# A recurrent and a deformable convolution stage on one core: bank order of the sampling tiles, a column-wise second depthwise convolution, and five linear chunks finished by ScalarE

## The reference

```
x = x + lstm_block(group_norm(x))      # over the 64 rows, both directions, 16 hidden units, then a linear layer
x = x + conv_block(group_norm(x))
conv_block(v):
    offset_a = conv1x1(relu(batchnorm(depthwise3x3(v))))           # a = x, y, 9 offsets for each pixel
    out_a[o,h,w] = sum over c, k of weight_a[o,c,k] * v[c] sampled at (h,w) shifted by offset_a[k] along a
    return relu(batchnorm(conv1x1(concat(conv3x3(v), out_x, out_y))))
```

## Time and profile before

| | |
|---|---|
| median of 3 runs | 857.25 us (857.21 to 860.83) |
| the profiled execution | 857.32 us, its span 855.5 us |
| PE / DVE / ACT / POOL busy | 86% / 72% / 57% / 29% of the span |
| recurrence | about 31 to 203 us |
| linear stage, norm | 204 to 237 us |
| convolutions, norm | 237 to 362 us |
| offset stage | 362 to 412 us |
| sampling loop | 413 to 829 us |

### The profile page before, as it was taken

The page is one execution under the profiler, slowest core; times in us unless marked ns, Lnnn a source line. Parts: engine busy times, 40 slices in busy tenths (PEclk is TensorE's granted clock), DMA queues, the critical chain, the costliest instruction groups (busy, mean ns, idle before and its releaser), DMA issues.

```text
span 855.5 us, 61033 instructions
## 1 busy us (share of the span) xinstructions
PE 737.8 (86%) x27560; PEld 589.2 (69%) x27560; DVE 615.3 (72%) x1136; ACT 487.8 (57%) x1001; POOL 248.9 (29%) x284
## 2 busy tenths in 40 slices
PE   0599999989499999499779999999999999999970
PEld 0455555555168899332469989998989998999960
DVE  4466666666913323666758989889889999999974
ACT  0344444443123333375657878788778787887844
POOL 1122222220000000000235344444454555555433
PEclk9999999999889999799999999999999999999995
DMA  8200000000000000000000000000000000000006
GB/s 232 88 3 1 0 0 0 0 2 1 3 3 5 4 4 5 3 1 1 3 4 0 0 0 0 0 0 0 0 0 0 0 0 0 0 0 0 0 2 196
DMA packets 4062, 11.97 MB, mean 14 GB/s; under 512 B 1391, under 2 KB 1787, under 8 KB 3460
## 3 DMA queue, kind: packets, MB, share of 16 engines
q1 hardware_dynamic: 1716, 4.88, 2.0%
q10 hardware_dynamic: 1522, 4.14, 1.7%
q0 software_dynamic: 768, 2.10, 0.9%
HBM read 6.92 MB, written 4.19 MB: 13 GB/s over the span
## 4 chain that ended last, share of the span: by engine, by line
PE 57%; DVE 17%; ACT 14%; issue 7%; DMA 2%; POOL 2%; ACTq 1%; DVEq 0%; POOLq 0%
PE psum L868 13%; PE psum L921 12%; PE psum L992 12%; PE psum L947 8%; ACT wide L485 6%; PE psum L939 5%; DVE wide L584 5%; DVE wide L587 4%; ACT wide L412 4%; PE psum L891 3%; ACT wide L408 3%; DVE offs L672 2%; DMA xs<-in_x_dram 2%; DVE xs L627 1%; DVE stats L618 1%
## 5 line engine op out<-in xcount | busy, mean ns | idle before, releaser
L485 ACT ACTIVATE wide<-psum 128x512 f32<-128x512 f32 x576 | 300.0, 601 | 16.4 <-PE psum L921 9.4
L921 PE MATMUL psum<-wide,sels 125*32 125x256 bf16 x4608 | 229.0, 274 | 0.5 <-ACT wide L485 0.2
L992 PE MATMUL psum<-wide 128*32 128x64 f32 x8192 | 192.6, 219 | 6.4 <-issue 6.4
L696 DVE TENSOR_SCALAR wide<-wide 128x1024 f32<-128x1024 f32 x256 | 180.6, 725 | 3.8 <-ACT wide L485 3.7
L992 PEld LDWEIGHTS psum<-wide 128*32 128x32 f32 x8192 | 167.1, 109 | 9.1 <-issue 7.5
L703 DVE COPY wide<-psum 128x1024 f32<-128x1024 f32 x128 | 155.9, 1218 | 2.0
L348 POOL COPY wide<-offs 125x256 bf16 (+1 forms) x64 | 26.9, 421 | 410.3 <-DVE offs L672 218.7
L340 POOL TENSOR_SCALAR wide<-wide 128x512 f32<-128x512 f32 x64 | 130.2, 2035 | 6.9 <-ACT wide L485 6.9
L868 PE MATMUL psum<-img,offs 32*32 32x512 f32 x3456 | 112.6, 611 | 5.8 <-ACT img L434 5.8
L947 PE MATMUL psum<-wc,wide 32*64 32x128 f32 x4096 | 112.1, 281 | 0.9 <-issue 0.9
L792 PEld LDWEIGHTS psum<-wide 128*64 128x64 f32 x2048 | 70.3, 137 | 61.1 <-DVE wide L595 60.1
(11 more groups left out here) (100 smaller groups left out, 769.5 us busy)
## 6 DMA issues: line engine op xcount, KB each, us to landing
xs<-in_x_dram ACTq DMA_DIRECT2D x8, 256.0 KB, 10.4
xs<-in_x_dram SPq DMA_DIRECT2D x8, 256.0 KB, 9.9
out_dram<-wide SPq DMA_DIRECT2D x16, 128.0 KB, 3.7
out_dram<-wide POOLq DMA_DIRECT2D x16, 128.0 KB, 4.2
offs<-in_cw_dram ACTq DMA_DIRECT2D x1, 576.0 KB
sels<-in_sel_dram ACTq DMA_DIRECT2D x1, 562.5 KB
wide<-in_dsc_dram ACTq DMA_DIRECT2D x1, 288.0 KB
offs<-in_dwd_dram ACTq DMA_DIRECT2D x1, 288.0 KB
```

The costliest lines, as they stand in the source:

```text
L485: nc.scalar.activation(hat_tile(par, i), use_bank(par, hat_use(i)).rearrange("p (q n) -> p q n", q=2), ACT.Abs).then_inc(d_read, 1)
L696: nc.vector.tensor_scalar(v, v, 1.0, 1.0, ALU.min, ALU.subtract).then_inc(v_ready, 1)
L921: last = mm(bank[c, e * SL:(e + 1) * SL], sels[:, k, c], oc[0:NROW, par, :], start=(e == 0), stop=(e == 1))
L992: last = mm(ps[O_BANK][C * q:C * q + C, cols], w, v, start=(group == 0), stop=(group == GROUPS - 1))
```

## The change

**Banks.** In even slots the three banks are taken backwards from 0 (0, 2, 1), in odd ones 2, 0, 1. Use 0 of every slot now waits for use 7 of the slot before, use 1 for use 9, use 2 for use 8.

**Columns.** `h_y` holds each image by columns. ACT reads the bank across its rows and writes runs of 8 for each column; the statistics read those runs; L891's successor (L920 and L921) reads plain stretches for both branches, for round `rd` the same numbers of columns as before. ACT rectifies by rounds of 2,048 columns, and both engines rectify the next round between the first part and the second of a round.

**Linear chunks.** Chunks 1, 4, 7, 10 and 13 get a second product, of an identity matrix in `avgs` with the residual, and ACT writes bank plus bias to `xs` (L435). The banks are three, 4 to 6. `avgs` grows from 128 to 192 KB.

```diff
         def use_bank(par, u):
-            return ps[(par * USES + u) % 3]
+            return ps[(0, 2, 1)[u % 3] if par == 0 else (2, 0, 1)[u % 3]]
         def use_free(par, u):
-            return (-1, 0, -2)[u] if par == 0 and u < 3 else u - 2
+            return (-2, 0, -1)[u] if u < 3 else u - 2
...
+        hyt = h_y.rearrange("p (b w h) -> p b w h", b=2, w=S)
+        def hy_chunk(n, rows=slice(0, P)):
+            r0 = n % (NCH // 2) * ROWS
+            return hyt[rows, n // (NCH // 2), :, r0:r0 + ROWS]
...
+        BY_ACT = tuple(range(1, NCH, 3))
...
+            for n in BY_ACT:
+                act.wait_ge(lin_ready, n + 1)
+                nc.scalar.activation(xv[:, :, 4 * n:4 * n + 4, :].rearrange("p b f t -> p f b t"),
+                                     ps[4 + n % 3][:, :].rearrange("p (f b t) -> p f b t", f=4, b=2), ACT.Identity,
+                                     bias=vecs[:, V_BLIN:V_BLIN + 1]).then_inc(x1_act, 1)
...
+                    def evacuate(own, at):
+                        src = conv_bank(m, i)[at, :]
+                        if j == 2:
+                            to, src = hy_chunk(n, own), src.rearrange("p (h w) -> p w h", h=ROWS)
...
+                    if done is part1[0] and rd + 1 < ROUNDS:
+                        relu_y_round(rd + 1)
...
-                        last = nc.vector.bn_stats(stats_hy[:, n, :], h_y[:, n * CH:(n + 1) * CH])
+                        last = nc.vector.bn_stats(stats_hy[:, n, :], hy_chunk(n))
...
+                    if done is part1[1] and rd + 1 < ROUNDS:
+                        relu_round(rd + 1)
...
             for n in range(NCH):
-                pe.wait_ge(x1_ready, 2 * n + 2)
-                mm(ps[4 + n % 2], wlin_s, seq[:, n * 4 * SEQ:(n + 1) * 4 * SEQ], start=True, stop=True).then_inc(lin_ready, 1)
+                if n >= 3:
+                    pe.wait_ge(x1_ready, 2 * by_dve(n - 3))
+                    pe.wait_ge(x1_act, by_act(n - 3))
+                last = mm(ps[4 + n % 3], wlin_s, seq[:, n * 4 * SEQ:(n + 1) * 4 * SEQ], start=True, stop=n not in BY_ACT)
+                if n in BY_ACT:
+                    last = mm(ps[4 + n % 3], avgs[:, 2, :], xv[:, :, 4 * n:4 * n + 4, :].rearrange("p b f t -> p f b t"),
+                              start=False, stop=True)
+                last.then_inc(lin_ready, 1)
...
-                pe.wait_ge(relu_y, b + 1)
+                pe.wait_ge(relu_y, rd + 1)
...
-                            rhs = hv[0][rows, b, r0, :] if a == 0 else hv[1][rows, b, :, r0].rearrange("p h w -> p w h")
+                            rhs = (hxv if a == 0 else hyt)[rows, b, r0, :]
```

More of the change, by code:

```diff
@@ L69, in build @@
         vecs = sb("vecs", [P, NVEC])
-        avgs = sb("avgs", [P, 2, P])
+        avgs = sb("avgs", [P, 3, P])
         sels = sb("sels", [NROW, NSEL, P], BF16)
@@ L229, in build, with by_act, by_dve @@
         FUSED_AT = K * C
+        BY_ACT = tuple(range(1, NCH, 3))
+        def by_act(n):
+            return sum(1 for m in BY_ACT if m <= n)
+        def by_dve(n):
+            return n + 1 - by_act(n)
         block = ctx.enter_context(nc.Block())
@@ L440, in _ @@
                     made_by, done = (conv_mm, conv_ev) if j == 0 else (hy_mm, hy_ev)
-                    to, bias = (acc, cbias) if j == 0 else (h_y, vecs[:, V_DWB + 1:V_DWB + 2])
-                    cols = slice(n * CH, (n + 1) * CH)
+                    bias = cbias if j == 0 else vecs[:, V_DWB + 1:V_DWB + 2]
+                    def evacuate(own, at):
+                        src = conv_bank(m, i)[at, :]
+                        if j == 2:
+                            to, src = hy_chunk(n, own), src.rearrange("p (h w) -> p w h", h=ROWS)
+                        else:
+                            to = acc[own, n * CH:(n + 1) * CH]
+                        return nc.scalar.activation(to, src, ACT.Identity, bias=bias[at, 0:1])
                     act.wait_ge(made_by, n + 1)
                     if i == PLACES[j]:
-                        last = nc.scalar.activation(to[:, cols], conv_bank(m, i)[:, :], ACT.Identity, bias=bias[:, 0:1])
+                        last = evacuate(slice(0, P), slice(0, P))
                     else:
@@ L468, in parts_x @@
                                              bias=vecs[0:ONE_ROW + 1, V_PWB:V_PWB + 1]).then_inc(done, 1)
+                    if done is part1[0] and rd + 1 < ROUNDS:
+                        relu_y_round(rd + 1)
             act.wait_ge(norm_done, BN + 1)
[L471 to L474, removed]
+            relu_y_round(0)
+            for rd in range(ROUNDS):
                 parts_x(rd)
@@ L619, in stats_x1 @@
                 return last
-            nc.vector.nop().then_inc(x1_ready, 4)
             for n in range(NCH):
[L624 to L628, removed]
-                        vecs[:, V_BLIN:V_BLIN + 1], xr, ALU.add, ALU.add).then_inc(x1_ready, 1)
+                if n not in BY_ACT:
+                    dve.wait_ge(lin_ready, n + 1)
+                    for b in range(2):
+                        xr = xv[:, b, 4 * n:4 * n + 4, :]
+                        nc.vector.scalar_tensor_tensor(
+                            xr, ps[4 + n % 3][:, :].rearrange("p (f b t) -> p b f t", f=4, b=2)[:, b],
+                            vecs[:, V_BLIN:V_BLIN + 1], xr, ALU.add, ALU.add).then_inc(x1_ready, 1)
                 if n % 2 == 0 and n > 0:
                     stats_x1(n // 2 - 1)
-            dve.wait_ge(x1_ready, 4 + 2 * NCH)
             step(stats_x1(NCH // 2 - 1))
```

19 lines of the change are left out of this document (8 added, 11 removed).

## The result

| | before | changed kernel |
|---|---|---|
| median | 857.23 us (857.04 to 860.83, 4 runs) | 846.03 us (843.39 to 846.42, 4 runs) |
| profiled execution, its span | 857.32, 855.5 us | 846.11, 844.2 us |

The ratio of the two is 0.9863 [0.9838, 0.9887]: faster, by 1.4% or 11.2 us where 13.8 were forecast, and inside the range. In a second comparison with more rounds it is 0.9878 [0.9851, 0.9906].

What follows compares the result with a forecast made beforehand. It took PE's bank waits in sampling, DVE in the linear stage and the PE-DVE chain in the offset stage as bounds. 6.3 + 5.2 + 2.6 = 14.1 us off 857.32 gave 843.2, say 843.5 us; range 838.5 to 851.

Steps and rivals of the forecast that it cites:

- What bounds the kernel: Claimed limits: PE's wait for ACT's bank in sampling, DVE in the linear stage, alternating PE and DVE in the offset stage.
- Banks: Sampling loop: even slots' project wait drops from 0.42 to 0.21 us, in 30 slots, 6.3 us gained.
- the banks do nothing in the second axis: Rival, sampling loop: bank order gains only in the first axis, as DVE has 0.29 us spare; 846.7 us, chance 0.06.
- Columns, offset stage: Offset stage: plain reads shorten L891, less relu now between parts; 0.2 + 1.6 + 3.4 = 5.2 us gained.
- the clock falling in some of the rounds: Rival, offset rounds: PE idles during relu, half of three L891 runs cold, costing 5.2 us; 848.7 us, chance 0.15.
- Y sets at one pass: Offset stage: with plain reads, weight loads of y sets come 0.43 us apart and L891 takes near 3.6 us.
- unchanged y sets: Rival, offset stage: y sets stay at 1.72 us because of tiles, not stride, losing 6.6 us; 855.0 us, chance 0.05.
- a clock low throughout: Rival, offset stage: PE stays at 1.2 GHz, making the stage 10.6 us slower; 859.0 us, chance 0.04.
- Convolutions: ACT's reads of PSUM across rows cost nothing; 0.2 us if doubled, 1.6 at four times the price.
- Linear stage: DVE gives five chunks to ACT but waits for chunk 2; the stage ends near 225.8, 2.6 us gained.
- Start: Load before the first norm: 64 KB more of avgs fit in the slack, cost nothing, or 0.3 us if x is delayed.

Runs made afterwards that it cites:

- f1: The changed kernel unmodified, run again on the chip of f2: 848.3 us, 0.9878 of the kernel before.
- c3: b4 with ACT's linear chunks at 2, 6, 9, 13 and 15 instead of 1, 4, 7, 10 and 13: 837.2 us.
- c4: b4 with the max of DVE's relu given to POOL in rounds 1 to 3: 838.7 us.
- f2: The changed kernel plus ten products of zeros on PE in a gap of each of the first three offset rounds: 842.2 us.
- f3: The kernel of c3 unmodified, run again with five rounds for its interval: 837.5 us.
- f4: c3 with POOL taking the max of DVE's relu in rounds 1 to 3 and ACT's relu at the head of its round: 831.6 us.
- b2: The kernel before with ACT's five linear chunks alone, including the third bank and larger avgs: 857.1 us.
- b3: The kernel before with the column-wise y branch alone, including relu between first and second part: 855.0 us.
- c2: The changed kernel with second-axis statistics over 8 elements of a partition instead of 512: 845.2 us.
- b4: The changed kernel with DVE's relu of the next round put back ahead of the first parts: 839.9 us.
- c1: The kernel before with only the y branch's 1x1 product reading plainly, in the wrong pixel order: 848.3 us.
- b1: The kernel before with the new bank order alone: 852.6 us.

## Why the prediction was right in sign and 2.5 us off in size

- **What bounds the kernel: right.** PE's wait for a bank in the sampling loop, DVE in the linear stage, the chain between PE and DVE in the offset stage were what moved.
- **Banks, -6.3 forecast, -5.99 measured (f1: -5.9).** The mechanism was right; that the number came out so near is luck, since two errors cancel. In the steady slots it is 0.30 and not 0.21 us for a pair in the first axis (6.49 to 6.19), which was my upper end, and 0.17 in the second, where DVE is the bound sooner than I had it; together 6.7 to 6.8. The wait before `project` fell by the 0.21 that I counted; to which row the other 0.09 of the first axis belong is open. Against that the first four slots take 35.18 us in the changed kernel and 34.86 in f1, where before has 34.57. In both the granted clock falls there, at 438.9 and 440.9, for 3.4 us; before doesn't show it. In the five profiles with the new order of banks and no fall there (c3, c4, f2, f3, f4) these slots take 31.8 to 33.2, in the five with it and a fall 33.7 to 35.2, in the three with the old order and no fall (before, b2, b3) 33.4 to 34.6. By the means of the three groups, 32.5, 34.5 and 34.0, an estimate is that the banks are worth 1.5 us more here, some 8 in all, and a fall takes 2 back; no kernel was made to test it. I had not looked at these slots beyond taking one off the count.
- **The rival that the banks do nothing in the second axis** fell, though over a third of the gain there is lost to DVE, as c2 shows (1.7 us of 4.5).
- **Columns, offset stage, -5.2 forecast, -3.45 measured. This is the term that was mis-sized:** "Rounds 1 and 2 ... 11.4 us", "Round 3 has no relu: 3.8 against 7.18" count every L921 but the first at 2.4 GHz. With the clock held up by f2's fillers the rounds are 12.93, 11.26, 11.25 and 9.78 where I had 13.2, 11.4, 11.4 and 9.85: that arithmetic was right to 0.3 us, and the stage would be 48.1, 5.7 less than before. What I gave a chance of 0.15, the clock falling in some of the rounds, is what happens, at 2.3 us (50.36 - 48.09) and not 5.2: two falls of 3.4 us each, in which PE's masks and the begin of L921 run at half speed, where I had counted half of three L921. The rule that I weighed, in the Trainium skill, TensorE: Matmul & The Clock Gate, HAM oscillation, speaks of bursts with gaps between them, there waits for DMA of some 3 to 5 us, behind which each burst starts cold. The trace agrees in two of the three rounds that have gaps (in c2 in all three), though PE's idle time here was not one gap of 2.5 us, as I had it, but two of 1.2. Where one of the two is filled (f2) or gone the clock doesn't fall: single gaps of 1.20 (b4, round 0), 1.26 (c4) and 1.59 us (c1) left it at 2.4 GHz. So it isn't the length of a gap alone; what of the two together brings the fall is open.
- **Y sets at one pass: right,** 0.43 us between weight loads, L921 3.67 us. The rivals of unchanged y sets and of a clock low throughout fell.
- **Convolutions, 0: right,** to 0.2 us; nothing of the 0.2 or 1.6 us that dearer reads of PSUM would cost. For ACT the rule of the Trainium skill, Advanced Engine Details and Errata, PSUM Cachelines, does not show; of matmuls no run here tells.
- **Linear stage, -2.6: right,** -2.4 in the changed kernel, -2.6 in L+C; the 1.70 us wait for chunk 2 stood where the working put it.
- **Start, 0:** +0.93 in the profile, and no run ties it to `avgs`. With the smaller `avgs` the first norm's matmul starts at 22.61, 21.90, 23.70 and 24.33 (before, b1, b3, c1), with the larger one at 22.96 to 24.03 in ten profiles. Between kernels with the same start it differs by up to 2.4 us; an effect of 0.3 can't be told in that.

What I missed altogether is the better place: the working priced the relu between the parts at 2.6 us a round and took it as part of the change. Ahead of the parts, where DVE waits for L921 anyway, it was worth 6.4 us more (b4).

What stays open: why the clock falls in the first slots of the loop in the changed kernel, f1, b1, b4, c1 and c2, and not in the kernel before, b2, b3, c3, c4, f2, f3 and f4. The profiles of both sorts show gaps of PE of over 1 us there. No run was made for it.

## What to carry to other kernels

When a step shortens the engine that was the cover for another one's work, look where that other work is to go now: here the relu belonged ahead of the parts, not behind the first, and when it no longer filled the round, the next engine's relu (ACT's) stood in the same wrong place. Two gaps of little more than a microsecond on PE, close together, can cost as much again through its clock; read the granted clock in windows of one us around every new gap, and price it in the forecast. Look also at the engine that you didn't move: here ACT's relu made one of the two gaps. Compare stretches between the same instructions, since the start alone scattered here by more than one part of the change was worth.

## What the runs showed of the hardware that I had not expected

- The clock falls behind pairs of gaps of 1.2 us on PE, in one round and not in the next with the same gaps (changed, f1, b3), or in all three (c2), and not behind single ones of 1.2 to 1.6 us (b4, c4, c1). Ten idle products in each of three rounds, 2.3 us of work each time, made the kernel 6.1 us faster in the median (848.3 to 842.2). In the profiles 2.5 of it is the offset stage and 2.0 the sampling loop; 1.8 is the start, which they can't have touched.
- Reading moving columns across rows (256 bytes apart) costs double at 2.4 GHz, 0.86 for 0.43 us a pass of 512 fp32 columns, and nothing at 1.2 GHz: in the first round at half clock DVE's first part came 3.78 us after the start of the 1x1 products before and 3.79 after (359.33 to 363.12).
- POOL takes 5.36 us by the profile, whose spans on POOL are rough, for a max over 128x2048 fp32 where DVE takes 1.23, and DVE's parts beside it stay at 6.05 for five.
- A good part of the scatter between runs of one kernel goes with PE's mean granted clock: f4 took 829.5 to 830.3 us in three runs at 0.973 and 832.9 to 834.9 in three at 0.966 to 0.969.
